# Attention inside a decoder block: the projections of the next pair of heads placed in two runs of a cycle instead of three

## The chip, the cores and the metric

One core of a Trainium2 chip runs the whole block in one program. The metric is the device time in microseconds; the kernel before took 1797.97 us, the median of 3 runs (1796.36 to 1801.69).

## The reference, cut to what matters

Input x is 4 batches of 1024 tokens by 256 features. Three sublayers follow each other, each with a residual and a layer norm:

```python
q = einsum('bnd,hde->bhne', x, Wq) / 8; k, v likewise     # 16 heads of 64
attn = softmax(einsum('bhne,bhme->bhnm', q, k))           # 1024 x 1024 per head
x = layernorm(x + (attn @ v, heads joined) @ Wp + bp)
x = layernorm(x + memory update)      # rows moved, a strided convolution of old rows
x = layernorm(x + top1_switch_ffn(x)) # 8 experts, capacity 128 tokens each
```

Everything is float32. Attention is by far the largest part: 64 (batch, head) pairs of 1024 x 1024 scores.

## The kernel before, in words

**Units, halves, quarters.** Heads are worked in pairs (32 pairs over 4 batches). A pair has two units of 512 queries, and a unit has eight key tiles kt of 128 keys. A unit is cut into two halves of four key tiles, so there are 128 halves h, and four halves, called quarters 0 to 3 here, make the cycle of one pair g = h // 4. Eight cycles are one batch.

**What a half holds.** For each of its four key tiles: a score (six matmuls of fp32r, high and low parts of q and k, the two heads in the upper and lower 64 rows of the array, L1214); its exp on ScalarE (L1325), which frees the score bank; a seed on ScalarE (L1336), which writes the negative row maxima into that bank so that the score two key tiles later is added onto them; an av on TensorE (probabilities of the half before times v, fp32, L1230); and an add on GpSimd (`prob_sum`, L1086, first one L1082). A unit needs seven adds. Its column total (`sum`, L1241) can be taken on TensorE only after the seventh. Every half also has four row passes, high parts of q and k only (L1190), whose maxima VectorE reads (L1395) for a unit that comes one or two halves later.

**Projections.** A bite (L1174 for q and k, L1167 for v) is one PSUM bank of q, k or v for the next pairs. ScalarE writes its high part (`high`, L1307, L1312), VectorE the low part of q and k (`low`, L1382). Six bites belong to a cycle: two of k at the end of quarter 0, one of v at the start of quarter 1, one of q near the end of quarter 2, and one of v and one of q in the middle of quarter 3. `bites_of` says which bites a quarter has; `STEPS` says where they stand.

**What sets the order.** `STEPS` has one line per quarter, a list of step names written out by hand. TensorE, ScalarE and VectorE each run through the same list and take the steps that are theirs, so the list fixes three program orders at once, and it fixes the rotation of the three spare PSUM banks (`SPARE`, L813) in which row passes (two banks each), bites, sums and the steps of the route live. A step waits for the last reader of its bank (`take`, L1138). The names `early` and `late` are two places per half where steps of the batch before are put: its output projection, norm 1, memory update, norm 2, router (`Route.plan`, L194). With s the half in the batch: s 3 to 10 have a projection `late` (with a split on ScalarE and on GpSimd), s 11 to 13 norm 1 on ScalarE, s 13 the `old` transposes, s 14 and 15 moves and their adds (`moved`) on GpSimd, s 15 `comp`, s 17 `scale`, s 18 to 22 norm 2, transposes and logits, s 23 `choose` early and `weigh` late on VectorE, s 24 `count`, s 27 `gate` early and `place` late on VectorE, s 28 `rows`, and from s 28 one `send` per half. SyncE and GpSimd don't follow `STEPS`: GpSimd does in each half the weight splits (L1059 to L1070, quarters 0 and 1), two adds, the early steps, two adds, the late steps.

**The DMA queue.** SyncE issues in quarters 1 and 3 the store of a unit's output, and in quarters 0 and 2 the round trip by which the row maxima reach all partitions. In s 14 it waits for norm 1 of all tiles (`x1_done`) and issues the moves of the memory update (L318), for which GpSimd's `add_moved` (L427) waits.

Of the kernel before, what the change touches and what calls it, by code (L numbers as in the profile page):

```python
# [34 lines left out]
class Route:  # L35
# [628 lines left out]

STEPS = tuple(tuple(line.split()) for line in (
    "av early av av pass score score exp exp pass sum av read read seed turn pass seed score score read exp pass recip exp read seed late bite bite high high low low seed",
    "bite norm high score exp pass score low read early pass exp av read seed seed av pass read score exp score pass read exp seed seed late av av",
    "av pass score exp score read exp pass seed av read seed sum pass score early turn read score recip exp pass read late bite exp seed high av seed av low",
    "pass read norm score exp score seed pass read exp bite high low seed bite av av high early low pass read score score exp exp pass late av read av seed seed"))


def bites_of(g, quarter, pairs):

    t, m = g // 2 + 1, 2 * (g % 2)
    planned = ((("k", g + 1, 0), ("k", g + 1, 1)), (("v", t, m),), (("q", g + 1, 1),),
               (("v", t, m + 1), ("q", g + 2, 0)))[quarter]
    return [(kind, of, n) for kind, of, n in planned if of < (pairs // 2 if kind == "v" else pairs)]


def build_attention(nc, x, Wq, Wk, Wv, oT_dram, xT_dram, shift_dram, const, route, probs, v, weights, block, signals):  # L680
# [33 lines left out]
    for g in range(PAIRS):  # L714
        for quarter in range(4):
            START_OF[4 * g + quarter] = len(BITES)
            BITES += bites_of(g, quarter, PAIRS)
            END_OF[4 * g + quarter] = len(BITES)
# [1446 lines left out]
```

## Time and profile before

| | value |
|---|---|
| median of 3 runs | 1797.97 us |
| the profiled execution itself | 1796.57 us |
| its span, first to last instruction | 1794.8 us |
| TensorE busy | 1728.4 us, 96% |
| GpSimd busy | 1383.5 us, 77% |
| ScalarE busy | 1299.0 us, 72% |
| VectorE busy | 1149.7 us, 64% |
| mean granted TensorE clock | 0.995 of full speed |

Attention runs from some 10 us to 1550 us of the span. The ends of matmuls are modelled, so short waits between two of them can be missing from the idle column; the distance between two starts is the sure measure.

### The profile page before, as it was taken

How to read it: one execution, taken by the hardware profiler on the slowest of the kernel's cores; microseconds unless marked ns; L12 is line 12 of the kernel's file. 1: busy time of each engine (PE TensorE's matmuls, PEld its weight loads, DVE VectorE, ACT ScalarE, POOL GpSimd, SP SyncE). 2: the span in 40 equal slices, each digit the busy share in tenths (PEclk: the TensorE clock that was granted, in tenths of full speed). 3: DMA queues.
4: the chain of work that ended last, by engine and by line, in shares of the span. 5: the costliest groups of instructions: out<-in, count | busy, mean ns of one | idle time of the engine just before them, and what ended most of it. 6: DMA issues, size and time to landing. Idle time of an engine off the chain costs nothing.

```text
span 1794.8 us, 29382 instructions
## 1 busy us (share of the span) xinstructions
PE 1728.4 (96%) x10380; PEld 1062.3 (59%) x10380; DVE 1149.7 (64%) x2122; ACT 1299.0 (72%) x1602; POOL 1383.5 (77%) x735
## 2 busy tenths in 40 slices
PE   6999999999999999999999999999999998999998
PEld 5555555555665555556655555556655554598887
DVE  5666666666556657766556667755566678675565
ACT  3687777777668777777667877776687877665674
POOL 2688888889887978899788878899888777641664
PEclk9999999999999999999999999999999999999999
DMA  4421111113312111133222111232222111633441
GB/s 135 144 61 42 48 42 48 42 48 99 131 52 79 48 42 48 45 107 128 70 69 67 42 48 42 57 100 77 65 70 67 54 39 56 198 109 127 144 142 36
DMA packets 142933, 137.72 MB, mean 77 GB/s; under 512 B 60741, under 2 KB 121285, under 8 KB 141765
## 3 DMA queue, kind: packets, MB, share of 16 engines
q1 hardware_dynamic: 139716, 127.38, 23.7%
q0 software_dynamic: 3072, 8.46, 1.3%
q8 instruction: 86, 1.41, 0.3%
q14 instruction: 59, 0.48, 0.1%
HBM read 102.70 MB, written 29.69 MB: 74 GB/s over the span
## 4 chain that ended last, share of the span: by engine, by line
PE 59%; POOL 24%; issue 7%; ACT 3%; DMA 3%; DVE 3%; SPq 1%; POOLq 0%; DVEq 0%; ACTq 0%
POOL prob_sum L1086 17%; PE av_ps L1230 15%; PE score_ps L1214 12%; PE spare_ps L1174 6%; PE spare_ps L1190 6%; PE y_ps L1816 4%; PE h_ps L1787 4%; PE spare_ps L1167 3%; PE spare_ps L1241 3%; PE spare_ps L446 2%; ACT probs L1325 2%; DMA x<-x 1%; DVE max_of L1395 1%; POOL prob_sum L1082 1%; POOL w_lo L1061 1%
## 5 line engine op out<-in xcount | busy, mean ns | idle before, releaser
L1086 POOL TENSOR_TENSOR prob_sum<-prob_sum,probs 128x1024 f32<-128x1024 f32 (+1 forms) x384 | 903.2, 2352 | 157.4 <-ACT probs L1325 122.7
L1395 DVE TENSOR_REDUCE max_of<-spare_ps 128x1 f32<-128x512 f32 x1024 | 655.2, 681 | 280.2 <-PE spare_ps L1190 275.9
L1325 ACT ACTIVATE probs<-score_ps 128x1024 f32<-128x1024 f32 x512 | 502.6, 1022 | 284.6 <-PE score_ps L1214 279.7
L1336 ACT ACTIVATE score_ps<-shift_all 128x1024 f32<-128x1024 f32 x510 | 511.3, 1030 | 1.1
L1230 PE MATMUL av_ps<-probs,v 128*64 128x512 f32 x2048 | 489.5, 603 | 0.5 <-ACT probs L1325 0.5
L1230 PEld LDWEIGHTS av_ps<-probs,v 128*64 128x64 f32 x2048 | 130.3, 136 | 242.7 <-issue 199.2
L1190 PE MATMUL spare_ps<-k_hi,q_hi 64*128 64x512 f32 x1024 | 231.3, 446 | 20.6 <-DVE max_of L1395 17.8
L1190 PEld LDWEIGHTS spare_ps<-k_hi,q_hi 64*128 64x128 f32 x1024 | 98.2, 184 | 224.1 <-issue 179.6
L1214 PE MATMUL score_ps<-q_hi,k_hi 64*128 64x512 f32 x1024 | 211.9, 409 | 3.7 <-ACT score_ps L1336 3.7
L1214 PE MATMUL score_ps<-q_hi,k_lo 64*128 64x512 f32 x1024 | 203.4, 392 | 0.0
L1214 PE MATMUL score_ps<-q_lo,k_hi 64*128 64x512 f32 x1024 | 202.6, 391 | 0.0
L1082 POOL TENSOR_TENSOR prob_sum<-probs 128x1024 f32<-128x1024 f32 (+1 forms) x64 | 150.6, 2354 | 59.3 <-ACT probs L1325 58.7
L1174 PE MATMUL spare_ps<-xT_kept,w_hi 128*128 128x512 f32 x496 | 155.4, 405 | 1.5 <-issue 1.0
L1214 PEld LDWEIGHTS score_ps<-q_hi,k_hi 64*128 64x128 f32 x1024 | 96.7, 185 | 42.9 <-ACT score_ps L1336 25.6
L1214 PEld LDWEIGHTS score_ps<-q_hi,k_lo 64*128 64x128 f32 x1024 | 97.1, 185 | 22.5
L1214 PEld LDWEIGHTS score_ps<-q_lo,k_hi 64*128 64x128 f32 x1024 | 97.2, 186 | 16.9
L1174 PEld LDWEIGHTS spare_ps<-xT_kept,w_hi 128*128 128x128 f32 x496 | 86.7, 190 | 30.6 <-issue 17.3
L1382 DVE SCALAR_TENSOR_TENSOR q_lo<-spare_ps,q_hi 128x512 fp32r<-128x512 f32 x62 | 42.9, 691 | 91.4 <-ACT q_hi L1312 90.0
L1167 PE MATMUL spare_ps<-wv_hi,xT_kept 128*128 128x256 f32 x488 | 91.1, 289 | 0.1
L1241 PE MATMUL spare_ps<-prob_sum,ones 128*64 128x512 f32 x256 | 68.8, 616 | 19.3 <-POOL prob_sum L1086 18.2
L1167 PEld LDWEIGHTS spare_ps<-wv_hi,xT_kept 128*128 128x128 f32 x488 | 72.9, 190 | 13.4 <-issue 11.1
L1174 PE MATMUL spare_ps<-xT_kept,w_lo 128*128 128x512 f32 x248 | 77.8, 395 | 0.0
(278 smaller groups left out, 2272.8 us busy)
## 6 DMA issues: line engine op xcount, KB each, us to landing
shift_all<-shifts SPq DMA_DIRECT2D x64, 512.0 KB, 4.0
o_transposed<-sums SPq DMA_DIRECT2D x64, 256.0 KB, 4.0
v<-in_L_ffn_W_dram SPq DMA_DIRECT2D x16, 1024.0 KB, 5.9
o_in<-o_transposed SPq DMA_DIRECT2D x28, 512.0 KB, 4.3
w_raw<-in_L_attn_Wq_dram SPq DMA_DIRECT2D x64, 64.0 KB, 3.0
w_raw<-in_L_attn_Wk_dram SPq DMA_DIRECT2D x64, 64.0 KB, 2.8
wv_raw<-in_L_attn_Wv_dram SPq DMA_DIRECT2D x32, 128.0 KB, 3.9
shifts<-neg_rows SPq DMA_DIRECT2D x256, 1.0 KB
```

The costliest lines, as they stand in the source:

```text
L1082: pool.tensor_tensor(out, probs[:, (n - 1) % RING, heads], probs[:, n % RING, heads], ALU.add).then_inc(prob_added, 1)
L1086: pool.tensor_tensor(out, out, probs[:, n % RING, heads], ALU.add).then_inc(prob_added, 1)
L1167: last = pe.matmul(bank[:, m * 4 * E:(m + 1) * 4 * E], xT[batch][:, half, kc, rows], w[:, kc, :], start=(i == 0 and kc == 0), stop=(i == 2 ...
L1174: last = pe.matmul(bank[:, :], w[:, of % 2, "qk".index(kind), kc, :], xT[batch][:, half, kc, cols], start=(i == 0 and kc == 0), stop=(i == ...
L1190: pe.matmul(bank[:, :], q_hi[rows, par, tokens], k_hi[rows, par, keys], start=True, stop=True).then_inc(pass_ready, 1)
L1214: last = pe.matmul(score_ps[n % 2][:, hd, :], a[rows], b[rows], start=(n < 2 and i == 0), stop=(i == len(products) - 1), skip_group_check= ...
L1230: last = pe.matmul(av_ps[hd * E:(hd + 1) * E, :], v[:, quad % 2, kt, 2 * first_head + hd, :], probs[:, n % RING, hd, :], start=(kt == 0), ...
L1241: last = pe.matmul(bank[hd * E:(hd + 1) * E, :], ones[:, 0:E], prob_sum[:, u % 2, hd, :], start=True, stop=True)
L1325: act.activation(probs[:, n % RING], score_ps[n % 2][:, :, :], ACT.Exp).then_inc(probs_ready, 1)
L1336: act.activation(score_ps[n % 2][:, :, :], shift_all[:, u % 2], ACT.Copy).then_inc(seeded, 1)
L1395: dve.tensor_reduce(max_of[:, u % 2, kh, j, hd:hd + 1], bank[:, :], AX.X, ALU.max).then_inc(pass_read, 1)
L1787: last = pe.matmul(h_bank(p, c)[:, rows], w[x][:, k, c * P:(c + 1) * P], xeT[y][:, k, rows], start=(i == 0 and k == 0), stop=(i == 2 and k ...
```

## The change: what it does

Three lines of `STEPS` and the table of bites. The v and the q bite of quarter 3 go to the end of quarter 2, behind the q bite that is there; quarter 3 has no bite. In quarters 2 and 3 the scores, avs and row passes are put in a new order around them: the `sum` of quarter 2 stands behind two avs instead of one, the first av behind the bites is one instead of two, and in quarter 3 the `late` place stands between the second pair of scores and the last row pass. In quarter 1 only the `late` place moves, to before the last seed.

```diff
 STEPS = tuple(tuple(line.split()) for line in (
     "av early av av pass score score exp exp pass sum av read read seed turn pass seed score score read exp pass recip exp read seed late bite bite high high low low seed",
-    "bite norm high score exp pass score low read early pass exp av read seed seed av pass read score exp score pass read exp seed seed late av av",
-    "av pass score exp score read exp pass seed av read seed sum pass score early turn read score recip exp pass read late bite exp seed high av seed av low",
-    "pass read norm score exp score seed pass read exp bite high low seed bite av av high early low pass read score score exp exp pass late av read av seed seed"))
+    "bite norm high score exp pass score low read early pass exp av read seed seed av pass read score exp score pass exp read seed late av seed av",
+    "av pass read score score exp seed exp seed pass av read av sum turn pass read recip score early score exp pass read exp late bite high seed low bite high low bite high low seed av",
+    "norm pass read score exp score exp seed seed pass read early av av pass read score exp score exp late seed seed pass read av av"))
 
 def bites_of(g, quarter, pairs):
     t, m = g // 2 + 1, 2 * (g % 2)
-    planned = ((("k", g + 1, 0), ("k", g + 1, 1)), (("v", t, m),), (("q", g + 1, 1),),
-               (("v", t, m + 1), ("q", g + 2, 0)))[quarter]
+    planned = ((("k", g + 1, 0), ("k", g + 1, 1)), (("v", t, m),), (("q", g + 1, 1), ("v", t, m + 1), ("q", g + 2, 0)),
+               ())[quarter]
```

## Rows read from the trace of the kernel before

**Rows 1.** The page: busy time, and the chain that ended last

```profile
PE 1728.4 (96%) x10380; PEld 1062.3 (59%) x10380; DVE 1149.7 (64%) x2122; ACT 1299.0 (72%) x1602; POOL 1383.5 (77%) x735
...
PE 59%; POOL 24%; issue 7%; ACT 3%; DMA 3%; DVE 3%; SPq 1%; POOLq 0%; DVEq 0%; ACTq 0%
```

**Rows 2.** Waits of TensorE: waiter, releaser, us in total, times, longest

```profile
PE spare_ps L1241 <- POOL prob_sum L1086: 18.2, 17, 2.1
PE spare_ps L1190 <- DVE max_of L1395: 17.8, 38, 2.5
```

**Rows 3.** Windows (stretch, us, busy by engine): quarters 2, 3, 0; quarter 3 at s 23, 27

```profile
245.24:255.00 9.76, 9.64 (x58) 4.81 (x55) 7.58 (x14) 8.09 (x9) 8.46 (x5) 1.00 0.01 2
255.00:268.44 13.44, 13.44 (x80) 7.29 (x78) 6.35 (x10) 8.72 (x10) 10.22 (x5) 1.00 0.27 80
268.44:278.71 10.27, 10.27 (x65) 6.73 (x62) 8.31 (x16) 8.54 (x10) 7.30 (x4) 1.00 0.01 1
...
679.65:693.38 13.73, 13.68 (x80) 7.18 (x78) 11.15 (x18) 8.86 (x11) 10.24 (x5) 1.00 0.35 96
724.02:737.46 13.44, 13.44 (x80) 7.17 (x78) 11.28 (x20) 8.71 (x10) 10.28 (x5) 1.00 0.25 78
```

**Rows 4.** Timeline of TensorE, 250 to 280: start, us, line, tile shape

```profile
251.26 0.70 PE L1174 MATMUL spare_ps<-xT_kept,w_hi 128*128 128x512 f32 x2
...
252.79 1.94 PE L1230 MATMUL av_ps<-probs,v 128*64 128x512 f32 x8
254.66 0.50 PE L1190 MATMUL spare_ps<-k_hi,q_hi 64*128 64x512 f32 x2
...
256.72 0.50 PE L1167 MATMUL spare_ps<-wv_hi,xT_kept 128*128 128x256 f32 x2
...
259.73 1.94 PE L1230 MATMUL av_ps<-probs,v 128*64 128x512 f32 x8
...
263.67 4.51 PE L1230 MATMUL av_ps<-probs,v 128*64 128x512 f32 x20
268.11 0.50 PE L1190 MATMUL spare_ps<-k_hi,q_hi 64*128 64x512 f32 x2
...
274.33 0.73 PE L1174 MATMUL spare_ps<-xT_kept,w_hi 128*128 128x512 f32 x2
...
278.71 0.50 PE L1214 MATMUL score_ps<-q_hi,k_hi 64*128 64x512 f32 x2
```

**Rows 5.** Timelines: ScalarE in the same cycle, GpSimd in h 6 and 7

```profile
269.35 1.94 ACT L1325 ACTIVATE probs<-score_ps 128x1024 f32<-128x1024 f32 x2 [2.69 <-PE score_ps L1214]
...
122.08 9.99 POOL L1086 TENSOR_TENSOR prob_sum<-prob_sum,probs 128x1024 f32<-128x1024 f32 x4
```

**Rows 6.** Timelines, s 13 to 16: ScalarE, SyncE, GpSimd, TensorE

```profile
571.42 1.08 ACT L351 ACTIVATE x<-x,shift,scale 128x256 f32<-128x256 f32 x2
...
572.53 4.18 SPq L318 DMA_DIRECT2D x<-x  x4
...
601.74 1.08 PE L1241 MATMUL spare_ps<-prob_sum,ones 128*64 128x512 f32 x4 [1.59 <-POOL prob_sum L1086]
```

**Rows 7.** Timelines of VectorE and GpSimd, s 23

```profile
683.16 0.99 DVE L594 TENSOR_TENSOR shifted_logits<-logits,top 128x64 f32<-128x64 f32 x1
...
684.69 2.02 DVE L600 TENSOR_TENSOR masks<-rank,first 128x64 f32<-128x64 f32 x1
...
681.66 4.97 POOL L1086 TENSOR_TENSOR prob_sum<-prob_sum,probs 128x1024 f32<-128x1024 f32 x2 [1.24 <-ACT probs L1325]
```

**Rows 8.** Timelines of VectorE, GpSimd, TensorE, s 27 of the last batch

```profile
1505.43 2.40 DVE L647 TENSOR_TENSOR work<-number,free_row 128x64 f32<-128x64 f32 x1
...
1508.12 2.25 DVE L649 SCALAR_TENSOR_TENSOR work<-number,work 128x64 f32<-128x64 f32 x1
...
1500.27 10.02 POOL L1086 TENSOR_TENSOR prob_sum<-prob_sum,probs 128x1024 f32<-128x1024 f32 x4 [0.83 <-ACT probs L1325]
...
1511.50 0.50 PE L1190 MATMUL spare_ps<-k_hi,q_hi 64*128 64x512 f32 x2 [2.53 <-DVE max_of L1395]
```

## The prediction

> **What bounds the kernel now.** I read the page first, then the waits, then the trace half by half. TensorE is busy 96% of the span and the chain that ended last lies 59% on it and 24% on GpSimd [rows 1]. So time moves in only two ways: TensorE's own stream gets shorter, or a wait in it appears or goes. Its two large waits are the sum that waits for GpSimd's last add and the row pass that waits for VectorE's read, 18 us each [rows 2]. Idle time elsewhere is worth nothing unless it turns into one of these.
>
> I cut the trace at the first score of each half. The pattern repeats to 0.1 us: without route work, quarter 2 takes 9.76 us, quarter 3 13.44, quarter 0 10.27 [rows 3]. Quarter 0 keeps its order, and so does TensorE in quarter 1, so quarters 2 and 3 carry the change: 23.20 us now.
>
> **TensorE's stream.** I measure runs from start to start [rows 4]. One q bite before avs: 252.79 - 251.26 = 1.53. Two avs and the change back to row passes: 254.66 - 252.79 = 1.87. Five: 268.11 - 263.67 = 4.44, so one av is (4.44 - 1.87) / 3 = 0.857 and a run of avs costs 0.16 on top. v and q bite together: 259.73 - 256.72 = 3.01. k, k, v: 278.71 - 274.33 = 4.38. A bite within a run is thus some 1.43, and each run of another tile shape adds about 0.1 to 0.17 us. A run "pass, score, score, pass" takes 2.06 (254.66 to 256.72), its first pass 0.34.
>
> Per cycle the old order has 18 such runs, the new one 17: one fewer entry into bites, one fewer from bites into avs, one more from passes into avs. New quarter 2, from its first score: 1.72 (rest of the run) + 2.73 (two avs and the sum) + 2.06 + 4.42 (three bites) + 1.02 (one av) + 0.34 = 12.29. New quarter 3: 1.72 + 1.87 + 2.06 + 4.44 + 0.34 = 10.43. Sum 22.72.
>
> The Trainium skill, "TensorEngine Tiling (Array Packing)", Key Properties, says that changing the tiling mode drains the engine; the trace agrees with some 0.15 us per change.
>
> **Waits in the quiet cycle.** Old quarter 2 has 0.34 of wait (9.76 against 1.72 + 1.87 + 2.06 + 1.53 + 1.87 + 0.34 = 9.4). It goes, since the sum stands 0.86 later. But where only two avs lie between two pairs of scores, ScalarE is late: two exps and two seeds take 3.9 us, and the second score of the pair comes 0.26 late. Quarter 0 shows it now: exps at 269.35 for scores at 268.44 [rows 5], and its window is 0.26 longer than its runs [rows 3]. New quarter 3 has this spacing (2.06 + 1.87), so 0.26 comes in: 22.98, against 23.20, a gain of 0.22.
>
> Three margins could take this back. The seed behind the third high part ends about 0.2 us before the second score of quarter 3 needs it. The row pass behind it waits for VectorE's read behind the norm; I get 0.1, hidden in the 0.26. GpSimd's last add: an exp starts 0.91 after its score and lasts 1.0, so the add of key tile 4 starts 2.0 us into quarter 3; four adds take 9.99 [rows 5], ready at 12.0; the sum of quarter 0 stands at 10.69 + 1.7 = 12.4. Margin 0.4. Quarter 3 now has 2.8 us less TensorE work over the same four adds; that is the cost of emptying it.
>
> **Quiet cycles:** the first batch has six (cycles 0 and 3 to 7): 6 x 0.22 = -1.3 us.
>
> **Cycles with projections** (cycles 0 to 2 of three batches): TensorE's route work is the same in both orders. Cycles 1 and 2 keep 0.2 each, 6 x 0.2 = 1.2. Cycle 0 of the second batch keeps nothing: a late step in quarter 3 now splits a run of passes (one more change of shape, 0.15), and the order exp, seed, exp in quarter 2 brings the first add there 1 us later, of which 0.1 reaches the sum. Net -1.1 (the other two cycles 0 come below).
>
> **First batch, cycles 1 and 2.** In h 6 and 7 GpSimd also splits Wp, twice 2.4 us. Adds run without a break from 122.08, where key tile 2 begins, so key tile 4 begins at 127.0 [rows 5]. The first score of h 6 stands at 114.0; in the new order the add of tile 4 can't start before 114.0 + 12.3 + 2.0 = 128.3. The rest of the chain is GpSimd's, so the sum in h 8 comes 1.2 us later. The sum in h 10, already bound by GpSimd and now with the extra av ahead of it, gives 0.77 back. +0.5.
>
> **Sum waits at s 30** (two batches, 1.6 to 1.7 us each, of the 18.2 [rows 2]): GpSimd sets that time, so the extra av in front of the sum is free: 0.77 gained each. 0.77 is what the stretch from the sum of quarter 2 to quarter 0 loses (old 1.0 + 2.06 + 1.53 + 1.87 + 0.34 + 13.44 = 20.24, new 0.98 + 2.06 + 4.42 + 1.02 + 0.34 + 10.69 = 19.5). At s 2 and 4 of the next batch GpSimd is still the bound, and its chain has come forward by 0.2 only, so 0.57 goes again. Net -0.4.
>
> **s 13 to 19.** In quarter 1 `late` now stands before the last seed. At s 13 this is norm 1 of two tiles: it ends at 572.5 and the moves are issued at 572.53, the moment it is done [rows 6]. It will end some 0.95 earlier, the seed that much later, which costs the second score of quarter 2 about 0.4. But the adds of the moved rows and a chain of ten GpSimd operations behind them hang on these DMAs, down to the sum that waits 1.59 at 601.74. It can come 0.95 earlier. With the sum at s 18 (0.3 of wait now) I get -1.1 a batch, three times: -3.3.
>
> **s 23.** `choose` is five small VectorE operations between the read of the second pass and that of the third. Two of them last 0.99 and 2.02 us where their likes last 0.22, and both end when an add of GpSimd ends: adds from 681.66, 4.97 for two, so boundaries near 684.1 and 686.6; the operations end at 684.15 and 686.71 [rows 7]. So `choose` lasts until the second add is over. Now two bites and two avs lie between pass 2 and pass 3; the fourth pass, which needs the bank of the third, waits 0.3. In the new order pass 4 stands 5.6 us after the first score, and the read of pass 3 is done at 6.95 (end of the adds) + 0.7 + 0.15 = 7.8. It waits 2.2. Price of the cycle: +2.0 for two batches. In the last batch the old order already loses 1.4 here (a bias add shifts the boundaries), and I expect +0.9. Together +4.9.
>
> **s 27.** `place` has three operations of the same kind, one per add boundary. In the last batch all four adds run without a break (10.02 us), two of its operations take 2.40 and 2.25, and the first pass of quarter 0 waits 2.53 [rows 8]. In the two batches before, quarter 3 has bites, GpSimd idles between adds (10.28 us busy in a window of 13.44), and no such wait exists (13.44 [rows 3]). The new order makes quarter 3 short there too: adds without a break until 11.8 us into the quarter, `place` ends with them, the read of pass 4 is done at 12.9, the pass that needs its bank stands at 10.5. +2.3, twice: +4.6. The last batch keeps its wait.
>
> The Trainium skill, "SBUF — State Buffer", "Who interferes with whom", has the rule for this: a `tensor_tensor` of VectorE with both inputs in SBUF contends with a GpSimd operation that reads SBUF, and the second waits in full. Rows 7 and 8 agree.
>
> **Sum:** -1.3 - 1.1 + 0.5 - 0.4 - 3.3 + 4.9 + 4.6 = +3.9 us. On the profiled execution's 1796.57 this is 1800.5. The median of the runs shown lies 1.4 above that execution: 1801.9 as a median. Bounds: `choose` and `place` cost nothing if their operations find a gap (-9.5, to 1792.4), and at most one more add each, 2.5 us for each of the five (+12, to 1814), which needs every phase to be bad; nearest is what rows 7 and 8 show. The move at s 13 is worth 0 to -3.3 (the wait behind it is 1.5 and TensorE follows within 0.9).
>
> **Rivals.**
> (A) VectorE's stalls don't come, because `choose` and `place` meet GpSimd between adds. For it: in s 27 of the second batch four of `place`'s operations take 0.22. Against: in the new quarter 3 the adds have no gap, since the fourth-tile add starts 2.0 us into it and 9.9 us follow. Time: 1801.9 - 9.5 = 1792.4, faster by 0.3%.
> (B) GpSimd becomes the bound of every cycle. Place: the sum in quarter 0. It decides from 0.4 us of delay on; if the first add of quarter 3 starts 0.8 late (adds stretch to 2.5, or an exp comes behind a seed), each of some 25 cycles loses 0.4: 1801.9 + 10 = 1812. For it: 24% of the chain is already there [rows 1]. Against: quarter 0 without route work shows only the 0.26 of the seed and no wait of the sum [rows 3], and the 0.4 are left by my count.
> (C) Only the quiet gain arrives and all route cycles are as before (the early norm gains nothing, no stall): 28 cycles by 0.22 = -6, 1792. It has the same sign as A and goes with it.
>
> **How the numbers follow.** My forecast 0.62, A and C together 0.18, B 0.20. What a measurement of this kernel can tell from no change is about 0.3%, 5.4 us: below 1792.6 or above 1803.4. Forecast: of 0.62, 0.45 within the bound, 0.15 above (its own range is 1797 to 1806), 0.02 below. A and C: 0.10 below, 0.08 within. B: 0.17 above, 0.03 within. So faster 0.12, within 0.56, slower 0.32. The range of 8 in 10 runs from 1793, most of A, to 1808, the near side of B.
>
> **What would show it.** In the new profile: quarter 2 near 12.3 and quarter 3 near 10.7 in quiet cycles; no wait of the sum in quiet quarter 0; a wait of pass 4 on the read of pass 3 of about 2 us in s 23 of three batches; a wait of the first pass of quarter 0 of 2.4 us after s 27 in three batches instead of one; moves issued 0.9 earlier relative to the half. It is wrong if the row pass waits stay at 18 us, or if sums wait in quiet cycles.

## The result and the profile after

The changed kernel took 1809.83 us (median of 5 runs, 1803.13 to 1811.61) against 1798.38 (5 runs of the kernel before): ratio 1.0059, interval 1.0042 to 1.0077. I had forecast 1801.9, a loss of 3.9 us that I called too small to tell, and a range up to 1808. The measured loss is 11.4 us by the medians, three times the forecast.

Its page, busy times and the chain that ended last, stands against [rows 1]:

```profile
PE 1739.5 (96%) x10380; PEld 1070.8 (59%) x10380; DVE 1158.6 (64%) x2122; ACT 1308.4 (72%) x1602; POOL 1384.0 (76%) x735
...
PE 68%; POOL 15%; issue 6%; DVE 5%; DMA 2%; ACT 2%; SPq 1%; POOLq 0%; DVEq 0%; ACTq 0%
```

TensorE has the same 10380 matmuls and is busy 11.1 us longer. That is the first sign: waits alone would not lengthen busy time. GpSimd's share of the chain fell from 24 to 15%. The waits of TensorE, against [rows 2]:

```profile
PE spare_ps L1190 <- DVE max_of L1395: 28.3, 42, 2.6
PE spare_ps L1241 <- POOL prob_sum L1086: 12.2, 11, 1.8
```

The waits for the sum fell by 6.0 us and those for VectorE's read rose by 10.5. Next the windows of quarters 2, 3 and 0 without route work, then quarter 3 of s 23, quarter 3 of s 27 and the quarter 0 behind it, all as in [rows 3] (the third number from the end of a line is the mean granted clock):

```profile
246.12:258.47 12.35, 12.35 (x74) 7.39 (x72) 8.07 (x15) 9.32 (x11) 9.88 (x5) 1.00 0.03 5
258.47:269.14 10.67, 10.67 (x62) 4.63 (x60) 5.75 (x10) 7.88 (x9) 7.93 (x4) 1.00 0.32 96
269.14:279.41 10.27, 10.27 (x64) 6.71 (x60) 8.29 (x16) 8.51 (x10) 8.16 (x4) 1.00 0.01 3
680.43:695.00 14.57, 12.40 (x64) 5.03 (x62) 10.63 (x18) 8.03 (x10) 11.32 (x6) 0.88 0.32 88
728.34:741.88 13.54, 10.91 (x64) 4.70 (x62) 13.18 (x19) 7.83 (x9) 9.59 (x4) 1.00 0.25 75
741.88:753.50 11.62, 11.62 (x66) 7.48 (x62) 8.84 (x20) 8.63 (x10) 6.35 (x3) 0.85 0.01 2
```

The quiet quarters are what I worked out: 12.35 (12.29), 10.67 (10.69), 10.27. So are the waits, 2.17 us at s 23 and 2.63 behind s 27. VectorE and GpSimd in these two halves of the second batch show what TensorE waited for:

```profile
683.85 1.02 DVE L594 TENSOR_TENSOR shifted_logits<-logits,top 128x64 f32<-128x64 f32 x1
...
685.42 2.02 DVE L600 TENSOR_TENSOR masks<-rank,first 128x64 f32<-128x64 f32 x1
687.47 1.29 DVE L1395 TENSOR_REDUCE max_of<-spare_ps 128x1 f32<-128x512 f32 x2
...
682.41 9.92 POOL L1086 TENSOR_TENSOR prob_sum<-prob_sum,probs 128x1024 f32<-128x1024 f32 x4 [3.20 <-ACT probs L1325]
...
688.31 0.80 PE L1190 MATMUL spare_ps<-k_hi,q_hi 64*128 64x512 f32 x2 [2.17 <-DVE max_of L1395]
...
735.46 2.39 DVE L647 TENSOR_TENSOR work<-number,free_row 128x64 f32<-128x64 f32 x1
...
738.14 2.25 DVE L649 SCALAR_TENSOR_TENSOR work<-number,work 128x64 f32<-128x64 f32 x1
...
730.29 10.02 POOL L1086 TENSOR_TENSOR prob_sum<-prob_sum,probs 128x1024 f32<-128x1024 f32 x4 [2.65 <-ACT probs L1325]
...
741.52 0.49 PE L1190 MATMUL spare_ps<-k_hi,q_hi 64*128 64x512 f32 x2 [2.63 <-DVE max_of L1395]
```

As in [rows 7, 8], VectorE's long operations end where an add of GpSimd ends, and now the four adds of quarter 3 run without a break in both halves. The moves of the memory update come as forecast too: they are issued 10.18 us after the first score of s 13 in the second batch (570.78 - 560.60), against 11.12 before (572.53 - 561.41).

What I did not have is the clock. The granted clock of TensorE has two levels in these traces, full (1.00) and half (0.50). In s 23 its mean is 0.88 over 14.57 us, in s 28 0.85 over 11.62: 0.12 x 2 x 14.57 = 3.5 us at half clock, and the same in s 28. It falls while TensorE waits or within 1.2 us of the wait's end. The two stretches cost 1.5 and 1.4 us: at full clock the same halves take 13.11 (s 23 of the last batch) and 10.29 (s 28 in e6 below). In [rows 3] the same quarter of s 23 has 1.00.

Where the span's 14.6 us (1809.4 - 1794.8) are, by the first score of each batch:

| stretch | before | after | difference |
|---|---|---|---|
| to the first score | 37.4 | 38.4 | +1.0 |
| first batch | 360.2 | 359.4 | -0.8 |
| second | 384.8 | 389.4 | +4.6 |
| third | 387.4 | 392.3 | +4.9 |
| fourth, to h 126 | 361.0 | 360.4 | -0.6 |
| tail | 264.0 | 269.5 | +5.5 |

### The profile page after: what moved, and what is told of

It reads as the page before. It is cut to its first block, busy times and chain, and to the rows that moved or that the text cites. A ratio compares the mean times of both kernels' runs of the same rounds, so it can differ in the third digit from the quotient of the medians.

```text
span 1809.4 us, 29377 instructions
## 1 busy us (share of the span) xinstructions
PE 1739.5 (96%) x10380; PEld 1070.8 (59%) x10380; DVE 1158.6 (64%) x2122; ACT 1308.4 (72%) x1602; POOL 1384.0 (76%) x735
## 4 chain that ended last, share of the span: by engine, by line
PE 68%; POOL 15%; issue 6%; DVE 5%; DMA 2%; ACT 2%; SPq 1%; POOLq 0%; DVEq 0%; ACTq 0%
PE av_ps L1230 17%; PE score_ps L1214 14%; POOL prob_sum L1086 11%; PE spare_ps L1174 8%; PE spare_ps L1190 7%; PE y_ps L1816 4%; PE spare_ps L1167 4%; PE h_ps L1787 4%; PE spare_ps L446 3%; PE spare_ps L1241 3%; DVE max_of L1395 2%; DMA x<-x 1%; POOL prob_sum L1082 1%; POOL expert_rows L435 1%; PE spare_ps L495 1%
## 5 line engine op out<-in xcount | busy, mean ns | idle before, releaser
L1190 PE MATMUL spare_ps<-k_hi,q_hi 64*128 64x512 f32 x1024 | 237.0, 456 | 29.5 <-DVE max_of L1395 28.3
L1425 DVE STREAM_TRANSPOSE sums<-spare_ps 128x512 f32<-128x512 f32 x64 | 45.6, 713 | 60.1 <-PE spare_ps L1241 60.1
```

The source lines that it names most:

```text
L1190: pe.matmul(bank[:, :], q_hi[rows, par, tokens], k_hi[rows, par, keys], start=True, stop=True).then_inc(pass_ready, 1)
```

## The experiments

Four questions: is the half clock caused by the waits; do the cycles of choose and place carry the loss; is the tail's 5.5 us the change's; is the part with the early norm (`late` of quarter 1 ahead of the last seed) worth what I said. A last run, e10, looks at what holds VectorE up. "Clock theory" in the expectations means that a wait is followed by a stretch at half clock.

**e4, waits of about 2 us put into the kernel before.** In quarter 3 of the eight cycles of the first batch:

```diff
+                if u % 2 == 1 and 3 <= u <= 17 and i == 2:
+                    for k in range(5):
+                        dve.tensor_reduce(held[:, 4 * k:4 * k + 4],
+                                          ones.rearrange("p (a n) -> p a n", a=1).broadcast_to([P, 4, P]), AX.X, ALU.max)
                 for hd, bank in enumerate(spare(("pass", u, i))):
```

> The kernel before with five extra VectorE reductions (about 0.68 us each, result unused) ahead of the read of pass 3 in quarter 3 of the eight cycles of the first batch, nothing else. Each makes pass 4 wait about 2.3 us. Rival (a wait costs its length): +18 us in all, quarter 3 at 15.7 us. Clock theory (a wait of more than 2 us is followed by a stretch at half clock): +25 to +28 us, the granted clock falls below 1 in at least six of the eight halves.

Measured: 1821.37 us, ratio 1.0133 (1.0118 to 1.0148), +23. The windows of its quarter 3 in h 7 and in h 11, each with the quarter 0 behind it:

```profile
127.60:143.10 15.50, 13.72 (x82) 7.20 (x80) 9.22 (x15) 9.68 (x12) 14.93 (x8) 1.00 0.31 86
143.10:153.30 10.20, 10.20 (x64) 6.69 (x60) 8.26 (x16) 8.48 (x10) 8.90 (x13) 1.00 0.01 2
173.80:191.00 17.20, 15.43 (x82) 7.56 (x80) 9.22 (x15) 8.71 (x10) 10.84 (x5) 0.90 0.19 62
191.00:201.20 10.20, 10.20 (x64) 6.68 (x60) 8.28 (x16) 8.51 (x10) 6.56 (x3) 1.00 0.01 2
```

The two are the same work with the same wait (1.78 us idle by the profile; the first is 2.05 longer than the 13.44 of [rows 3]). In the second TensorE is busy 1.71 us longer for the same 82 matmuls, at a mean clock of 0.90. Of the eight places four took 15.5 and four 17.2. So 8 x 2.05 + 4 x 1.7 = 23.2, the measured loss. Both theories missed: a wait costs its length always, and another 1.7 us in half of the cases. In the other traces none of these eight quarters has half clock, so the inserted waits are what brought it; what decides in which four is not shown.

**e8, shorter waits.** The same with `range(3)`.

> The kernel before with three extra reductions instead of five ahead of the same eight reads. Each wait is about 0.7 us, 8 x 0.7 = +5.5 us. Clock theory: a wait this short brings no half clock in any of the eight halves, quarter 3 near 14.2 us in all of them. Rival (any wait can bring it, in proportion): at least one or two of the eight halves are 1.7 us longer than the others, total +8 or more.

Measured: 1804.02, ratio 1.0034 (1.0024 to 1.0044), +6.5. The eight cycles are 0.9 us longer each and alike (14.30 to 14.32 for quarter 3), and no half clock falls in any of them, as the clock theory said. The same trace has one elsewhere, at s 30 of the second batch behind a wait of 1.77 us for the sum; that half takes 13.00 us instead of 11.40.

**e6, the changed kernel again.**

> The changed kernel once more, unchanged. If the stretches at half clock behind the waits are caused by them, at least two of s 23 and s 28 in batches 2 and 3 show them again, and the median is 1807 to 1812. If they were chance, none or one of the four does. For the tail behind attention (269.5 us against 264.0 in the first two profiles): if the change makes it longer, it is again over 268 us; if it is chance, it may fall anywhere from 264 to 270.

Measured: 1806.48, ratio 1.0045 (1.0030 to 1.0061). Windows at s 23 of the three later batches, and s 28 of the second and third:

```profile
680.40:695.00 14.60, 12.41 (x64) 5.08 (x62) 10.97 (x18) 8.36 (x10) 11.33 (x6) 0.88 0.24 63
741.90:753.50 11.60, 11.60 (x63) 7.61 (x64) 8.82 (x19) 8.37 (x10) 6.09 (x3) 0.85 0.01 2
1072.50:1087.00 14.50, 12.31 (x68) 4.96 (x66) 11.28 (x18) 9.29 (x11) 10.79 (x7) 1.00 0.30 92
1134.00:1145.70 11.70, 11.60 (x76) 8.08 (x76) 9.47 (x21) 9.54 (x12) 7.54 (x4) 1.00 0.01 3
1466.00:1480.80 14.80, 12.62 (x64) 5.08 (x64) 10.18 (x17) 7.77 (x10) 11.83 (x5) 0.88 0.04 13
```

(The two windows at full clock reach over the end of their half: by its scores that s 23 takes 13.11 and that s 28 10.29.) Three of the places have half clock, against four in the first profile, and one of the three, s 23 of the last batch, had full clock there. Of the four places that the expectation names, two have it again. The median is just below the 1807 I expected, and the tail took 267.2, below the 268 that stood for a tail made longer by the change.

**e7, the new order only in cycles 5 and 6 of the later batches**, where choose and place are:

```diff
+def renewed(g):
+
+    batch, cycle = divmod(g, 8)
+    return batch > 0 and cycle in (5, 6)
...
+    if renewed(g):
+        planned = ((("k", g + 1, 0), ("k", g + 1, 1)), (("v", t, m),), (("q", g + 1, 1), ("v", t, m + 1), ("q", g + 2, 0)),
+                   ())[quarter]
...
+        steps = (NEW_STEPS if renewed(h // 4) else STEPS)[h % 4]
```

> The kernel before with the new order only in cycles 5 and 6 of the last three batches (s 20 to 27, where choose and place are). Theory (these six cycles carry the loss): waits of 2.2 and 2.6 us as in the changed kernel, +10 us of waits and 3 to 6 us of half clock, so +12 to +16 us, more than the whole change. Rival (the loss is spread over the other cycles too): +3 to +7 us.

Measured: 1812.37, ratio 1.0077 (1.0056 to 1.0098), +14.9. TensorE's waits for reads are those of the whole change:

```profile
PE spare_ps L1206 <- DVE max_of L1411: 28.3, 42, 2.6
PE spare_ps L1257 <- POOL prob_sum L1102: 17.8, 17, 2.1
```

Six cycles of 32 cost more than the change as a whole (+9.0 in e6, +11.4 in the first runs), so the other 26 gain. All three s 23 had half clock, and one of the s 28. Its tail, with these waits in the same places, took 264.0.

**e5, the new order only where it is shorter**, with the new line of quarter 1 everywhere:

```diff
+    batch, cycle = divmod(g, 8)
+    return cycle > 2 if batch == 0 else cycle in (1, 2, 3, 4, 7) and g < 30 or g == 8
```

> The new order only in the cycles where the two profiles show it shorter (first batch 3 to 7; later batches 1 to 4 and 7, and cycle 0 of the second), the old order in the cycles of Wp, choose and place and in the last two, and the quarter 1 line of the change everywhere. Theory (the change gains 0.2 to 1.3 us in each such cycle and its whole loss is the waits at s 23 and s 27 with the half clock behind them): 7 to 9 us faster than the kernel before, about 1790. Rival (the gains are given back in the next cycle that GpSimd bounds, or each switch of order costs): 3 us faster at most.

Measured: 1793.79 (12 runs) against 1797.49, ratio 0.9979 (0.9968 to 0.9990): 3.7 us faster than the kernel before and faster than the changed one, by about half of what I expected. In its profile the batches take 359.0, 382.1, 385.7 and 360.1, so attention is 6.4 us shorter than in the profile of before. The halves say where the rest went: cycle 7 gains 0.7 twice and the cycle 0 behind it, in the old order there, loses 0.9 twice, since GpSimd sets both (the rival's mechanism); and cycle 2 gains 0.2 in the third batch, where the whole change gained 1.3, and loses 0.2 in the fourth. Its tail is 2.2 us longer than that of before; what more lies between 6.4 and the medians' 3.7 was not traced. The waits, against [rows 2], are 5.1 us less for the sum:

```profile
PE spare_ps L1206 <- DVE max_of L1411: 17.8, 38, 2.5
PE spare_ps L1257 <- POOL prob_sum L1102: 13.1, 12, 2.4
```

**e1, only the line of quarter 1** in the kernel before (`seed seed late av av` becomes `seed late av seed av`).

> The kernel before with only the quarter 1 line of the change (late ahead of the last seed). Theory A (the move of norm 1 at s 13 lets the moves, the ten GpSimd operations behind them and the sum at s 16 come about 1 us earlier in three batches): half s 16 goes from 11.6 to 11.0 us or less, s 14 grows by 0.1 to 0.4, total -1.5 to -3.3 us. Rival (the gain of s 16 comes from the new quarter 3 and not from this line): s 16 stays within 0.2 us, total 0 to +1.

Measured: 1795.57 (12 runs), ratio 0.9989 (0.9979 to 0.9999), 2 to 2.7 us less, at the edge of the noise; the halves show it clearly. Half s 16 takes 10.65, 10.53 and 10.55 instead of 11.71, 11.59 and 11.64, and s 14 grows by 0.14 to 0.17. The sum there, against [rows 6]:

```profile
600.86 1.08 PE L1241 MATMUL spare_ps<-prob_sum,ones 128*64 128x512 f32 x4 [0.54 <-POOL prob_sum L1086]
```

The wait fell from 1.59 to 0.54. The theory of the early norm holds and its rival is out.

**e2, the change without that line.**

> The changed kernel with the quarter 1 line of before, so only the moved bites and the new quarters 2 and 3. If the early norm is worth what I think, this is 1.5 to 3.3 us slower than the changed kernel; the waits of 2.2 us in s 23 and 2.6 us in s 27 stay as they are in all three batches. Clock theory (each of those waits is followed by a stretch at half clock that costs 1.1 to 1.3 us more): s 23 again near 14.6 us and s 28 near 11.7 in batches 2 and 3. Rival (the half clock stood there by chance in one execution): at least two of these four places show full clock, s 23 near 13.1 and s 28 near 10.6.

Measured: 1809.42, ratio 1.0063 (1.0051 to 1.0076). In its trace cycles 3 and 4 together take 0.8 to 0.9 us longer than in the changed kernel in each later batch, so some 2.5 us in all; the medians don't resolve that beside the clock. Half clock in all three s 23 (14.81 us), in neither s 28 (10.28, 10.30). So two of the four places that the expectation names are at full clock: as many as the rival asked for, although s 23 has it every time. It took e4 to show that waits cause it.

**e3, the same bites with the reads ahead of choose and place.**

```diff
-    "norm pass read score exp score exp seed seed pass read early av av pass read score exp score exp late seed seed pass read av av"))
+    "norm pass read score exp score exp seed seed pass read av av pass read score exp score exp early pass read late av av seed seed"))
```

> The changed kernel with quarter 3 in another order: the early steps (choose at s 23, gate at s 27) behind the read of pass 3 and the late ones (place at s 27) behind the read of pass 4, so that no row pass has its bank behind them. Theory (VectorE operations held up by GpSimd's adds delay the reads, and the waits that follow cost their length plus half clock): the waits of 2.2 and 2.6 us go or shrink below 1.1 us, no half clock in s 23 and s 28, total 8 to 12 us below the changed kernel, less about 2 us for the steps that now split runs of avs at other places. Rival (the change is slow for another reason, the waits are paid back elsewhere): less than 4 us below the changed kernel.

Measured: 1806.3, ratio 1.0043 (1.0030 to 1.0056), 3.5 us below the changed kernel's first median and no better than its second, e6: the rival. The waits moved on. s 23 is 10.75 without half clock, but s 24 waits 0.88 and 0.6; `place` now holds the first reads of s 28, which wait 2.0:

```profile
PE spare_ps L1190 <- DVE max_of L1395: 22.7, 42, 2.3
PE spare_ps L1241 <- POOL prob_sum L1086: 16.0, 15, 2.7
...
PE spare_ps L495 <- ACT x2T L380: 2.4, 3, 0.8
```

Waits of 2 us for the sum in s 4 of two batches brought half clock as well (16.5 us instead of 14.8), and so did the 2.0 at one s 28. Once a shorter one did: s 19 has a wait of 0.8 us for `x2T` in all three batches, and in the last half clock follows (15.73 us instead of 14.0).

**e9, the new order only in the last two cycles**, for the tail (`return g > 29`).

> The kernel before with the new order only in the last two cycles (g 30 and 31), which hold one bite and none. In the two profiles of the changed kernel and in the two of its variants the tail behind attention took 267 to 270 us, in six kernels that end in the old order 264 to 270. If the new order of the last cycles makes the tail longer, this is 2 to 3.5 us slower than the kernel before. If the tail's length is chance (how long TensorE is granted half clock around 1600 us), it is within 1 us.

Measured: 1798.15 (12 runs), ratio 1.0004 (0.9993 to 1.0014). The new order in the last two cycles does not make the kernel slower. The spread of the tail stands in the windows around 1600 us, where TensorE works on the router of the last batch: the changed kernel, e8 (old order) and e7:

```profile
1600.00:1620.00 20.00, 18.32 (x104) 17.88 (x102) 11.24 (x31) 10.73 (x21) 1.05 (x2) 0.66 0.17 54
```

```profile
1600.00:1620.00 20.00, 18.32 (x103) 17.88 (x103) 11.00 (x31) 10.19 (x20) 0.00 (x0) 0.66 0.15 53
```

```profile
1600.00:1620.00 20.00, 18.32 (x127) 17.50 (x126) 13.78 (x37) 15.05 (x30) 6.83 (x7) 0.91 0.42 131
```

0.34 x 2 x 20 = 14 us at half clock in the first two, 3.6 in the third; their tails take 269.5, 269.7 and 264.0. The tails of all twelve profiles lie between 263.8 and 269.7 and go with their time at half clock (its last stretch, in the final 3 us of every profile, left out): 3.4 us in the three shortest (before, e7, e9: 263.8 to 264.0), 13.7 in the three longest (269.5 to 269.7). The four with the whole change or e3's variant are 267.2 to 269.7, the eight others 263.8 to 269.7: the tail's 5.5 us in my pair of profiles are half clock and mostly chance, and a small part of it may not be.

**e10, three tiny VectorE operations beside a running add**, in the kernel before, at the read of pass 2: in four cycles `tensor_tensor` on two slices of an SBUF tensor, in four `tensor_reduce` on one.

> The kernel before with three tiny VectorE operations (28 columns, result unused) ahead of the read of pass 2 in quarter 3 of the eight cycles of the first batch: in four of them a tensor_tensor with both inputs in SBUF, in the other four a tensor_reduce with one input in SBUF. GpSimd has an add running there. Port theory: of each three two-input operations at least one lasts until the add ends, 0.5 to 2.4 us, and none of the twelve one-input ones lasts over 0.3 us. Rival (VectorE is slow there for another reason, small operations as such or semaphore traffic): both kinds last alike.

Measured: 1803.58 us (one run). From its trace: all operations of the first line (count, duration in ns as least, median, most), those of the second, then two of the groups of three with the adds beside the later one:

```profile
L1397 DVE TENSOR_TENSOR held<-ones x12: 174/176/2358, 126.3 to 393.5; 128x28 f32<-128x28 f32 x12
```

```profile
L1399 DVE TENSOR_REDUCE held<-ones x12: 170/172/175, 83.2 to 348.2; 128x1 f32<-128x28 f32 x12
```

```profile
83.23 0.35 DVE L1399 TENSOR_REDUCE held<-ones 128x1 f32<-128x28 f32 x3
...
126.30 1.45 DVE L1397 TENSOR_TENSOR held<-ones 128x28 f32<-128x28 f32 x3
...
125.11 4.92 POOL L1087 TENSOR_TENSOR prob_sum<-prob_sum,probs 128x1024 f32<-128x1024 f32 x2
```

The twelve with one input all take 0.17 us; with two, each group of three loses 1.1 to 2.2 us once, and 126.30 + 1.45 = 127.75 is where the first add ends (125.11 + 4.92 / 2 = 127.6). So the port theory of the expectation holds. The two kinds also differ as operations, but the kernel before rules that out: `low` is a two-input VectorE operation with one input in PSUM, and none of its 62 on q was held:

```profile
L1382 DVE SCALAR_TENSOR_TENSOR q_lo<-spare_ps,q_hi x62: 690/691/693, 37.8 to 1496.9; 128x512 fp32r<-128x512 f32 x62
```

The same operation with both inputs in SBUF (L649, [rows 8]) lasts 2.25 us beside an add, on 64 columns.

## Why the prediction was wrong

Point by point, from the halves of the two profiles ("measured" is the difference in us between the changed kernel's first profile and that of before):

| step | forecast | measured | at full clock |
|---|---|---|---|
| quiet cycles | -1.3 | -1.0 | -1.0 |
| cycles with projections | -1.1 | -2.6 | -2.6 |
| Wp, cycles 1 and 2 | +0.5 | +0.4 | +0.4 |
| sums at s 30, and cycle 0 behind | -0.4 | +0.5 | +0.5 |
| s 13 to 19 | -3.3 | -3.8 | -3.8 |
| s 23 | +4.9 | +8.5 | +5.5 |
| s 27 and the quarter 0 behind | +4.6 | +7.8 | +5.0 |
| last cycles | 0 | -1.4 | 0.0 |
| sum | +3.9 | +8.4 | +4.0 |

The last column takes the half clocks out: four of the changed kernel (s 23 at 13.11, s 28 at 10.3) and one of the kernel before, at s 28 of the last batch (9.38 us; 7.98 at full clock). It comes out at the sum I predicted. That it does so to 0.1 us is luck, since errors of up to 1.5 us cancel: cycles with projections gained 1.5 more (I had given cycle 2 just 0.2, and in the third batch it gave 1.3, since its sum had waited 1.25), and the sums at s 30 lost 0.5 where I had a gain. Every other row is within 0.6 us. (In the item on s 30 the gain is 20.24 - 19.5 = 0.73 by its own terms, not 0.77.)

**The step that failed** is the price of a wait. "It waits 2.2. Price of the cycle: +2.0" and "+2.3, twice" take a wait of TensorE at its length. The waits were there, 2.17 to 2.19 and 2.63 to 2.64 us. With them the granted clock was halved for a stretch, at a further 1.4 to 1.7 us. Over the four profiles that have them (the changed kernel twice, e2, e7) this happened in 10 of 12 places at s 23 and in 4 of 8 at s 28. e4 shows it in a kernel without the change, 4 of 8, and e8 shows waits that lengthen the quarter by 0.9 us without it. In the first pair of profiles the four stretches cost 5.8 us, 4.4 when the one that the kernel before has is taken off. So 4.4 of the 9.0 to 11.4 us (e6 and the first runs) are half clock; 4.0 are the waits and gains that I had; the other 1 to 3 us are the tail, which I had put at nothing, and the spread of the clock elsewhere, which the runs don't divide further.

I had the rows for it: the page of before has a mean clock of 0.995, and I read that as full clock, without asking what stood before the stretches that make the 0.005. One of them stands right behind the wait of 2.53 us that [rows 8] shows at 1511.50. This is s 28 of the last batch, in the kernel before and in the changed one, where the wait is 2.63:

```profile
1511.80:1521.18 9.38, 7.34 (x41) 4.08 (x40) 7.81 (x17) 6.82 (x8) 2.94 (x3) 0.82 0.01 2
```

```profile
1522.47:1530.45 7.98, 5.92 (x40) 3.27 (x37) 7.76 (x16) 6.70 (x8) 2.93 (x3) 1.00 0.01 2
```

The same work takes 1.4 us more at the lower clock. At this place five of the six profiles with the old order in that cycle have half clock (all but e10, which takes 7.98), and none of the five with the new order (the changed one twice, e2, e7, e9). Why is not shown.

**Rivals.** A (no stalls) is out, since the waits came. B (GpSimd bounds every quarter 0) is out in quiet cycles, whose quarter 0 took 10.27 with no wait for the sum; it is right for cycle 0 of the third and fourth batches, where s 4 waits 1.82 instead of 1.2. C (only the quiet gain) is out by the waits and by the 3.8 us that s 13 to 19 gained.

**What e5 adds.** The change's mechanism is good for some 0.2 to 1.3 us in most cycles; with the six cycles of choose and place left in the old order (and, for smaller reasons, the first three cycles, cycle 0 of the last two batches and the last two cycles) it is faster than the kernel before.

## What to carry to other kernels

A wait put into a stream that was full can cost more than its length on TensorE: e4 paid 23 us for waits that lengthened its quarters by 16, e8 6.5 for 7. Whether several short waits are cheaper than one long one of the same sum was not run; these two point that way, and e3's wait of 0.8 us warns against counting on it. Before a wait is priced by its length, look at the granted clock behind the waits that the kernel already has. When a part of a hand-written order is emptied, look for what was hidden behind the work that left: here tiny two-input VectorE operations that GpSimd's adds hold until their end. An order need not be the same in every cycle: choose it per cycle, by which steps share it.

## What the runs showed of the hardware that I had not expected

- The same wait at the same place of a cycle brings a stretch at half clock or doesn't: in e4 four quarters of 15.5 us and four of 17.2, all with 1.77 to 1.80 us of idle time. Length alone does not decide: the waits of 2.3 and 2.4 us for the sum in e5 (s 2 of the last two batches) brought none, one of 0.8 us in e3 did.
- The end of the kernel varies by 6 us in profiles of kernels that are the same there, by how long half clock lasts in it: a clock of 0.66 or 0.91 over the same 20 us around 1600.
- A VectorE `tensor_tensor` over 28 columns takes 0.174 us or 2.36, by what GpSimd has begun; `tensor_reduce` beside the same adds never more than 0.175.
